# A transformer layer with 64 experts: the last stage keeps its first sum in the product's bank and takes the statistics of a tile between the sums of the next

## What is computed

```python
x = x + _layernorm(_attn(_layernorm(x)))
x = x + _layernorm(_moe(_layernorm(x)))

def _moe(x):
    ...
    routed = zeros((T + 1, h)).at[buf_tok.reshape(-1)].add(eo.reshape(-1, h))[:T]
    shared = silu(xf @ shared_gate_w.T) * (xf @ shared_up_w.T) @ shared_down_w.T
    return routed + shared
```

## Time and profile before

| what | value |
|---|---|
| median of 3 runs | 1968.72 us (1955.16 to 1973.68) |
| the profiled execution, its own time | 1969.8 us |
| its span, first to last instruction | 1967.8 us |
| busy over the span: TensorE, VectorE, ScalarE, GpSimd | 92%, 74%, 53%, 28% |
| last stage, 1757 us to the end: adds of the residual (L1413), 64 | 94.6 us busy, mean 1500 ns |
| last stage: second sum (L1349), 64 | 58.2 us busy, mean 910 ns |
| last stage: first sum (L1347), 64 | 43.5 us busy, mean 680 ns |
| last stage: statistics (L1353), 64 | 44.5 us busy, mean 695 ns |

### The profile page before, as it was taken

The page is one execution under the profiler, slowest core; times in us unless marked ns, Lnnn a source line. Parts: engine busy times, 40 slices in busy tenths (PEclk is TensorE's granted clock), DMA queues, the critical chain, the costliest instruction groups (busy, mean ns, idle before and its releaser), DMA issues. The chain is left out here.

```text
span 1967.8 us, 53720 instructions
## 1 busy us (share of the span) xinstructions
PE 1804.6 (92%) x16329; PEld 1410.4 (72%) x16329; DVE 1458.7 (74%) x3876; ACT 1039.1 (53%) x2257; POOL 548.1 (28%) x772
## 2 busy tenths in 40 slices
PE   5899999999999999999999999966799999978886
PEld 3688888888888888888888888753455555556564
DVE  6688888888888888888888888844344444439897
ACT  4576667676767676766666666621233323223333
POOL 1021212121212121212121212111344444437777
PEclk8799999999999999999999999977899999999999
DMA  6355565656565656565566656476999999979994
GB/s 221 82 146 161 151 170 149 170 149 171 148 170 148 169 149 170 153 165 154 165 154 164 163 156 171 119 191 222 293 306 307 288 293 299 290 233 387 403 385 162
DMA packets 549277, 400.85 MB, mean 204 GB/s; under 512 B 424873, under 2 KB 433193, under 8 KB 549161
## 3 DMA queue, kind: packets, MB, share of 16 engines
q1 hardware_dynamic: 528672, 341.77, 59.3%
q0 software_dynamic: 14336, 35.66, 7.7%
q10 hardware_dynamic: 6208, 22.68, 3.1%
HBM read 249.24 MB, written 150.63 MB: 203 GB/s over the span
## 5 line engine op out<-in xcount | busy, mean ns | idle before, releaser
L935 POOL TENSOR_SCALAR ve<-mv 128x1 f32<-128x1 f32 x192 | 43.1, 225 | 986.1 <-DVE mv L758 986.1
L644 ACT COPY kT<-bank 48x256 f32<-48x256 f32 x512 | 307.9, 601 | 12.6
L1140 PE MATMUL e_gu<-w,xgT 128*128 128x384 f32 x512 | 187.3, 510 | 20.7 <-issue 11.1
L473 PE MATMUL bank<-wgu,xfT 128*128 128x416 f32 x512 | 188.9, 369 | 6.5 <-ACT xfT L644 5.6
L644 ACT COPY qT<-bank 48x256 f32<-48x256 f32 x512 | 187.7, 367 | 12.6 <-PE bank L466 1.6
L474 PE MATMUL bank<-wgu,xfT 128*128 128x416 f32 x512 | 182.8, 357 | 0.0
L1301 DVE SCALAR_TENSOR_TENSOR tanh<-tanh,e_gu 128x192 f32<-128x192 f32 x64 | 22.6, 354 | 174.9 <-ACT tanh L1227 174.9
L1140 PEld LDWEIGHTS e_gu<-w,xgT 128*128 128x128 f32 x512 | 94.2, 194 | 80.3 <-issue 20.3
L1384 POOL DMA_INDIRECT acc_scratch<-eo,sidx x64 | 101.5, 1586 | 128.8 <-ACT eo L1223 112.0
L644 ACT COPY probT<-score_ps 128x512 f32<-128x512 f32 x128 | 75.2, 588 | 112.0 <-PE score_ps L466 112.0
L1163 PE MATMUL e_ps<-w,hidT 96*128 96x512 f32 x256 | 127.0, 618 | 1.6 <-ACT hidT L1215 0.9
(11 more groups left out here) (178 smaller groups left out, 4789.2 us busy)
## 6 DMA issues: line engine op xcount, KB each, us to landing
w<-w_eg SPq DMA_DIRECT2D x60, 768.0 KB, 6.5
acc_scratch<-zero SPq DMA_DIRECT2D x130, 256.0 KB, 4.0
w<-w_ed SPq DMA_DIRECT2D x60, 384.0 KB, 10.5
xf_scratch<-xf SPq DMA_DIRECT2D x64, 288.0 KB, 2.1
xin<-x SPq DMA_DIRECT2D x64, 256.0 KB, 3.0
x_raw<-xt SPq DMA_DIRECT2D x64, 256.0 KB, 3.3
v_scratch<-v SPq DMA_DIRECT2D x64, 256.0 KB, 3.5
vbd<-v_scratch SPq DMA_DIRECT2D x128, 128.0 KB, 3.2
```

The costliest lines, as they stand in the source:

```text
L473: nc.tensor.matmul(dst, a[:, 0], b[:, 0], start=(n == 0), stop=False)
L644: nc.scalar.copy(dst, src).then_inc(done.sem, 1)
L1140: last = nc.tensor.matmul(gu_ps[par], xgT[:, par, n, :], w1[:, place, n, :], start=(n == 0), stop=(n == KD - 1))
```

## The change

In the last stage:

- The first sum goes back into the bank of the product (`sh_ps[n]`), and the second sum adds `acc2` to it and writes `acc`. TensorE's `down` waits for the second sum of the group before instead of the first.
- Statistics and aggregate of a tile are taken during the next tile: between the two sums of the next tile stands the bn_stats, and behind its second sum the aggregate. `st` has one buffer per tile of a group for it. The aggregate waits for the roots of group g-2 (`roots`), where bn_stats waited for that group's normalise.
- ScalarE normalises group g-2 in body g instead of g-1, and stores g-3 instead of g-2. GpSimd's bodies are shifted by one group too.
- In the first stage the two bias semaphores become one, and DVE waits for all five loads at tile 0.

```diff
             def down(g, n):
                 pe.wait_ge(s_hT.sem, s_hT.at(g * 2 + n))
-                pe.wait_ge(v_y.sem, v_y.at(g * 2 + (n - 2), 1))
+                pe.wait_ge(v_y.sem, v_y.at(g * 2 + (n - 2)))
...
-                if not isinstance(g, int) or g > 0:
-                    normalise(g - 1, (u - 1) % NR)
                 if not isinstance(g, int) or g > 1:
-                    store(g - 2, (u - 2) % NR)
+                    normalise(g - 2, (u - 2) % NR)
+                if not isinstance(g, int) or g > 2:
+                    store(g - 3, (u - 3) % NR)
...
-            def total(g, u, n):
-                y = acc[:, u, n * D:(n + 1) * D]
+            def add_first(g, u, n):
                 dve.wait_ge(p_sh.sem, p_sh.at(g * 2 + n))
                 dve.wait_ge(acc_in[u].sem, acc_in[u].at(g))
-                nc.vector.tensor_tensor(y, sh_ps[n], y, ALU.add).then_inc(v_y.sem, 1)
+                nc.vector.tensor_tensor(sh_ps[n], sh_ps[n], acc[:, u, n * D:(n + 1) * D], ALU.add).then_inc(v_y.sem, 1)
+
+            def add_second(g, u, n):
                 dve.wait_ge(v_y.sem, v_y.at(g * 2 + n, 1))
-                nc.vector.tensor_tensor(y, acc2[u][:, n * D:(n + 1) * D], y, ALU.add).then_inc(v_y.sem, 1)
+                nc.vector.tensor_tensor(acc[:, u, n * D:(n + 1) * D], sh_ps[n], acc2[u][:, n * D:(n + 1) * D],
+                                        ALU.add).then_inc(v_y.sem, 1)
+
+            def stats(g, u, n):
                 dve.wait_ge(v_y.sem, v_y.at(g * 2 + n, 2))
-                dve.wait_ge(a_norm.sem, a_norm.at(g - 2))
                 settle(dve)
-                nc.vector.bn_stats(st[:], y).then_inc(v_y.sem, 1)
-                dve.wait_ge(v_y.sem, v_y.at(g * 2 + n, 3))
+                dve.wait_ge(v_s.sem, v_s.at(g * 2 + (n - 2)))
                 settle(dve)
-                nc.vector.bn_aggr(mv[:, u % 2, n, :], st[:]).then_inc(v_y.sem, 1)
+                nc.vector.bn_stats(st[:, n], acc[:, u, n * D:(n + 1) * D]).then_inc(v_s.sem, 1)
+
+            def moments(g, u, n):
+                dve.wait_ge(v_s.sem, v_s.at(g * 2 + n, 1))
+                dve.wait_ge(roots.sem, roots.at(g - 2))
+                settle(dve)
+                nc.vector.bn_aggr(mv[:, u % 2, n, :], st[:, n]).then_inc(v_s.sem, 1)
 
             def body(g, u):
+                later = not isinstance(g, int) or g > 0
                 low_part(g, 1)
-                total(g, u, 0)
+                add_first(g, u, 0)
+                if later:
+                    stats(g - 1, (u - 1) % NR, 1)
+                add_second(g, u, 0)
+                if later:
+                    moments(g - 1, (u - 1) % NR, 1)
                 if not isinstance(g, int) or g + 1 < NG:
                     low_part(g + 1, 0)
-                total(g, u, 1)
+                add_first(g, u, 1)
+                stats(g, u, 0)
+                add_second(g, u, 1)
+                moments(g, u, 0)
...
             def body(g, u):
+                if not isinstance(g, int) or g > 1:
+                    residual(g - 2, (u - 2) % NR)
                 if not isinstance(g, int) or g > 0:
-                    residual(g - 1, (u - 1) % NR)
-                invert(g, u)
+                    invert(g - 1, (u - 1) % NR)
...
                 if isinstance(i, int) and i == 0:
-                    dve.wait_ge(latent_bias_in, 16)
-                if isinstance(i, int) and i == 1:
-                    dve.wait_ge(biases_in, 16 * 4)
+                    dve.wait_ge(biases_in, 16 * 5)
```

More of the change, by code:

```diff
@@ L257, in token_pipeline @@
         part_in = [sem(f"part_in{n}") for n in range(len(parts))]
-        latent_bias_in = sem("latent_bias_in")
         biases_in = sem("biases_in")
@@ L363, in _ @@
                 if n == KD - 1:
-                    sp.dma_start(blat[:], b_lat.partition_broadcast(P)).then_inc(latent_bias_in, 16)
+                    sp.dma_start(blat[:], b_lat.partition_broadcast(P)).then_inc(biases_in, 16)
                     load_x(1, 1)
@@ L988, in experts_and_norm @@
         eo = sb("eo", [P, NW, D])
-        st = sb("f_st", [P, 6])
+        st = sb("f_st", [P, G, 6])
         mv = sb("f_mv", [P, 2, G, 2])
@@ L1047, in experts_and_norm @@
         v_hT = tiles("f_v_hT")
-        v_y = tiles("f_v_y", 4)
+        v_y = tiles("f_v_y", 2)
+        v_s = tiles("f_v_s", 2)
         roots = groups("f_roots", 4)
@@ L1255, in body @@
                     high_part(g + 1, 0)
-                if not isinstance(g, int) or g > 0:
-                    normalise(g - 1, (u - 1) % NR)
                 if not isinstance(g, int) or g > 1:
-                    store(g - 2, (u - 2) % NR)
+                    normalise(g - 2, (u - 2) % NR)
+                if not isinstance(g, int) or g > 2:
+                    store(g - 3, (u - 3) % NR)
             high_part(0, 0)
             ring(act, body)
+            normalise(NG - 2, NR - 2)
+            store(NG - 3, NR - 3)
             normalise(NG - 1, NR - 1)
@@ L1365, in _ @@
+                stats(g, u, 0)
+                add_second(g, u, 1)
+                moments(g, u, 0)
             low_part(0, 0)
             ring(dve, body)
+            stats(NG - 1, NR - 1, 1)
+            moments(NG - 1, NR - 1, 1)
         @block.gpsimd
@@ L1394, in invert @@
                 k = u % 2
-                pool.wait_ge(v_y.sem, v_y.at(g * 2 + 1))
+                pool.wait_ge(v_s.sem, v_s.at(g * 2 + 1))
                 pool.wait_ge(a_norm.sem, a_norm.at(g - 2))
@@ L1415, in body @@
             def body(g, u):
+                if not isinstance(g, int) or g > 1:
+                    residual(g - 2, (u - 2) % NR)
                 if not isinstance(g, int) or g > 0:
-                    residual(g - 1, (u - 1) % NR)
-                invert(g, u)
+                    invert(g - 1, (u - 1) % NR)
             ring(pool, body)
+            residual(NG - 2, NR - 2)
+            invert(NG - 1, NR - 1)
             residual(NG - 1, NR - 1)
```

## The result

| what | before | after |
|---|---|---|
| median | 1968.14 us (1955.16 to 1975.81, 10 runs) | 1947.32 us (1940.54 to 1955.01, 10 runs) |
| ratio, 95% interval | | 0.9906 [0.9884, 0.9928] |
| span of the profiled execution | 1967.8 us | 1945.4 us |
| last stage, first sum of tile 0 to the end | 210.1 us (from 1757.7) | 191.3 us (from 1754.1) |

By the ratio the change makes the kernel 0.9% faster, some 18.5 us; the two medians lie 20.8 us apart. The forecast was 1946, 1.2% less than before. The last stage alone is 18.8 us shorter. It also begins 3.6 us earlier, but this is not the change's: over all executions that were profiled for this study (the experiments among them) the stage began between 1743.2 and 1760.4, whatever the kernel.

A forecast was written before the change was run, and what follows sets the result against it. GpSimd's and ScalarE's loop, 6.25 us a group, was taken as the bound. Roots of group 1 at 1772.7, plus 30 x 5.40, plus 8.7 give span 1943.4, 24.4 less: 1945.4, say 1946 us; range 1938 to 1962.

The forecast's parts named there:

- The exclusion: Last stage: a DVE instruction with two SBUF inputs and GpSimd exclude each other, costing GpSimd 0.51 + 0.39 us per group.
- the ring: Last stage, GpSimd and ScalarE: roots, normalise, two residual adds, next roots; from 6.25 to 5.35 us a group.
- DVE's tile: Last stage, DVE's work on one tile: 2.49 us with statistics between the sums, where it was 2.95.
- The rival that the gaps stay: Last stage, DVE: gaps ahead of the statistics remain, 3.00 us a tile, time 1960 us; chance 0.11.
- The start: Beginning of the last stage: roots of group 0 at 1765.7 us, roots of group 1 at 1772.7.
- The period: Steady groups of the last stage: 5.40 us each, 30 of them from roots of group 1 to roots of group 31.
- Hidden, with 9 us left: Last stage, later refills: routed rows land 24 us after a normalise and are needed at 33 us, so nothing waits.
- DVE waiting for acc_scratch: Last stage: sign that the forecast is wrong, if DVE waits for these transfers after 1760 us.
- The rival of the transfers: Last stage: transfers bind, 67.3 MB ahead of the last load's end; time 1935 or 1954 us; chance 0.13.
- Normalise behind the casts: Last stage, ScalarE: casts hold up normalise in every group, 7.0 us a group, time 1993 us; chance 0.07.
- Not on the path: Last stage, ScalarE: casts ahead of a waiting normalise cost nothing, given 0.4 us of idle DVE per group.
- The biases: First stage, one bias semaphore: costs nothing, since the last bias lands at 25.0 us, just in time; at most 8 us.

The follow-up runs named there:

- The first experiment: Kernel before with only the two sums changed (first into the product's bank, second from it; TensorE waits for the second): 1950.4 us, ratio 0.992.
- the second experiment: Kernel after with both sums in SBUF again and TensorE waiting for the first sum, the new order kept: 1951.44 us, ratio 0.9927.
- the roots ahead: Kernel after with GpSimd taking the roots of group g-1 ahead of the residual adds of g-2: 1940.51 us, ratio 0.987.
- the third experiment: Kernel before with only the two bias semaphores merged, all five biases waited for at tile 0: 1965.34 us, ratio 0.9998.
- the lighter x: Kernel after with only an eighth of each x refill loaded from group 8 on: 1937.04 us, ratio 0.9851.

## Why the prediction was right, and where it was not

**The exclusion** was read rightly. Adds 2.54 a pair (2.48 forecast from the quiet end; so 0.06 more with other engines at work beside them), L1421 at 0.20, the ring at 5.35. That it fits to the hundredth is luck in part: the roots follow the adds by 0.09 instead of 0.15, which makes up for the 0.06. The first experiment shows the mechanism alone. By the Trainium skill (SBUF — State Buffer, Who interferes with whom), a DVE instruction with at most one SBUF input, outside the 2-port perf modes, doesn't contend with GpSimd; the 64 even second sums agree. What the prediction took for the price of an exclusion, 0.51 + 0.39 us of GpSimd, was the price in one order of starts: in the second experiment GpSimd pays 0.32 of it, and the rest is on DVE, where it was free. "One instruction and GpSimd exclude each other" was right; that GpSimd pays it all depended on the order, and my expectation for that run failed on this.

**DVE's tile** was forecast at 2.49 and took 2.35. Both statistics and second sum start 0.60 behind the instruction ahead, as the row of L1294 suggested, and the new first sum costs its 0.70 in length but only 0.60 in distance, since nothing waits for its end. The rival that the gaps stay (3.00) is out. The new first sum was forecast at 0.75 and took 0.70. DVE was to be busy near 80%; it is at 89% from 1800 to 1850 (44.62 of 50 us), and the forecast's own sum, 2 x 2.49 of 5.40, had it at 92%.

**The start** went as written: from the first sum the roots of group 0 come at +7.9 (forecast 7.95), the first normalise at +11.1 (11.35), the roots of group 1 at 1768.76, +14.6 (14.95).

```profile
1761.97 0.23 POOL L1417 TENSOR_SCALAR f_ve<-f_mv 128x2 f32<-128x2 f32 x1 [16.45 <-DVE f_mv L1364]
...
1765.18 1.52 ACT L1242 ACTIVATE f_acc<-f_acc,f_shift,f_rstd 128x512 f32<-128x512 f32 x2
```

**The period** is the term that failed. Forecast was 30 x 5.40 = 162 us; the roots of group 31 came at 1936.78, 168.0 after those of group 1: 6 us more. The tail was 8.6 for 8.7. The span came out at 1945.4 for 1943.4 only since the stage began 3.6 us earlier than that of the kernel before (6.0 - 0.3 - 0.1 - 3.6 = 2.0). Without this luck the profiled span would have been 1949, and the shorter stage alone (18.8 us off the median of 1968.1) gives 1949 too. That the median of 1947 lies so close to the forecast of 1946 is in part luck.

The step behind it is "Hidden, with 9 us left". It took 11.6 us for a landing, from the start of the stage in the kernel before, and kept it for a stage that asks for more per us. It also looked at the routed rows, which DVE needs, and not at the hidden rows, which TensorE needs at the head of a group: the sign that it named, DVE waiting for acc_scratch, never came, and TensorE waited for h_scratch instead. The issues of the kernel after, from 1825 to 1865 and from 1885 to 1910, show otherwise (two landings of 18.6 are 37 us, over the 33 that it had):

```profile
f_h<-h_scratch SPq DMA_DIRECT2D x7, 384.0 KB, 16.1
```

```profile
f_h<-h_scratch SPq DMA_DIRECT2D x4, 384.0 KB, 17.7
w<-acc_scratch SPq DMA_DIRECT2D x4, 512.0 KB, 18.6
out<-f_res ACTq DMA_DIRECT2D x4, 512.0 KB, 6.8
```

and the stretches show that the rate did not rise with the demand:

```profile
1800.00:1850.00 50.00, 46.77 (x223) 36.43 (x222) 44.62 (x95) 21.10 (x36) 36.75 (x57) 1.00 1.03 414
1850.00:1900.00 50.00, 41.81 (x202) 32.17 (x201) 40.46 (x83) 21.03 (x35) 33.36 (x53) 1.00 1.03 414
```

At 5.35 us a group the stage asks for 2.490 MB / 5.35 = 465 GB/s and gets 414. The buffers' lead makes up for the difference for about 20 groups; then the pace is 6.02 us, measured 6.10. Before, at 6.25, the demand was 398 GB/s, below what is moved here, and hidden rows landed in 6.5 us (1885 to 1927). How much lead there is can be estimated from two kernels: 0.67 us a group are short for 19 groups in the kernel after, 12.7 us, and 1.20 for 12 groups with the roots ahead, 14.4 us. By this estimate 32 groups can go at about 5.6 us without a hole, and the second experiment did, at 5.67. A change that brings the ring far below that can't be paid in full.

**The rival of the transfers** was right in its mechanism and wrong in its sum. Its last load was to be in at 1918.8 at 416 GB/s, 161.8 us into the stage. The very last load, an x issued at 1909.41, landed at 1925.8, 171.7 us into it, since from 1754 to 1800 only 383 GB/s were moved. The last hidden rows landed at 1921.6, 167.5 us into it:

```profile
1921.64 0.55 PE L1177 MATMUL e_ps<-c,f_h 128*128 128x128 f32 x3 [1.12 <-DMA f_h<-h_scratch]
```

but behind them the sum had 14.4 us (two tiles on DVE and the last group), and it took 1945.4 - 1921.6 = 23.8: hidden rows are used at the head of a group's work, so both products, the sums and almost two periods of the ring come behind them. With 23.8 instead of 14.4 the rate below which transfers decide is 67.3 MB / (1943.4 - 23.8 - 1757) = 414 GB/s, not 391: almost the upper of the two rates that it knew, 373 and 416. So the rival deserved far more than 0.13. The Trainium skill (DMA: Bandwidth & Descriptors, Specifications) has about 358 GB/s for a core at the HBM, which it works out as half of a stack's 716 GB/s for two cores. This kernel runs on one core, and 414 held here for 100 us, so the figure doesn't bound it. By that figure, as an estimate, 67.3 MB take 188 us, and with the 23.8 behind them the span would have ended at 1969.

**Normalise behind the casts**, the slower rival, did not come with its price, 7.0 us in every group: by the timelines ScalarE's normalise starts 0.1 us behind the roots in the steady groups. But its mechanism is how the transfers cost time. From group 20 on the casts are late because the hidden rows are, and the normalise behind them starts 0.9 to 2.3 us behind the roots in six groups. So the forecast's "Not on the path" holds only as long as the rows are in time, and its sign of being wrong, over 0.2 us in more than the first groups, did show. **The biases** cost nothing that the third experiment could show.

## What to carry to other kernels

When two engines exclude each other, find out which one starts first and whether the other has time to wait: giving one operand a home in PSUM removes the cost, and moving the start can put most of it on an engine that has time. Before counting on a shorter period, divide the bytes of one period by the highest rate that the trace holds; if the new period is below that, the buffers' lead pays the difference for some periods (here 13 to 14 us in all), and the rest is lost. Look at what stands behind a late load in each queue: here a normalise that needed none of it. Of a load that binds, count what comes behind the use of it, which for the input at the head of a stage is more than a tile of the engine that ends it.

## What was not expected of the hardware

- The exclusion goes to whoever has started: the second sum ran 1.70 us when it started inside an add, and it held L1417 for 0.32 in turn (second experiment). It is held by the instruction, not shared in time.
- The landing time of the hidden rows on SyncE's queue grew from 6.4 us (1754 to 1800) and 11.7 (1800 to 1825) to 16.1 (1825 to 1865) and 17.7 (1885 to 1910), while the rate stood at 414 GB/s from 1800 on; the stores on ScalarE's queue stayed at 6.7 to 7.2. So in a backlog one queue can be late and another not.
- Issuing itself becomes slow in a backlog: the issue of w took a median of 2.77 us and up to 3.94, with the lighter x 0.45. From 1850 on SyncE waits for no semaphore in the kernel after; it only issues.
- A sum from a PSUM bank back into it, 128x512 in float32, takes 0.70 us, and with its output in SBUF 0.68.
